# Decoder block on one core: the product of the triangular inverse with the scores, cut to the 64 rows that are used

## The reference, cut to what matters

```python
def step(S, inp):
    qt, kt, vt, gt, bt = inp
    S = S * jnp.exp(gt)[..., None, None]
    kv = jnp.einsum('bhk,bhkv->bhv', kt, S)
    delta = (vt - kv) * bt[..., None]
    S = S + jnp.einsum('bhk,bhv->bhkv', kt, delta)
    o = jnp.einsum('bhk,bhkv->bhv', qt, S)
    return (S, o)
```

## Time and profile before

| | before |
|---|---|
| time, median of 3 executions | 2269.97 us (2269.26 to 2271.44) |
| span of the profiled execution, first to last instruction | 2267.6 us |
| mean granted TensorE clock | 0.981 |
| PE busy | 2108.4 us (93%) |
| DVE busy | 1704.1 us (75%) |
| ACT busy | 1397.1 us (62%) |
| POOL busy | 833.0 us (37%) |

### The profile page before, as it was taken

How to read it: one execution, slowest core, us unless ns; L and a number is a source line. 1 busy time by engine, 2 the same in 40 slices (tenths; PEclk the granted TensorE clock), 3 DMA queues, 4 the chain that set the end, 5 groups by cost and what they waited for, 6 DMA issues and landing times.

```text
span 2267.6 us, 81281 instructions
## 1 busy us (share of the span) xinstructions
PE 2108.4 (93%) x33098; PEld 1786.0 (79%) x33130; DVE 1704.1 (75%) x5291; ACT 1397.1 (62%) x4262; POOL 833.0 (37%) x1845
## 2 busy tenths in 40 slices
PE   4899999999999999999999999999999999999976
PEld 3688888788888888888888788878888878887864
DVE  4577777777777777878777778777778777777743
ACT  3575556776556776555776555776555776555642
POOL 3333334433334433334433334433334433334421
PEclk8799999999999999999999999999999999999997
DMA  6000000000000000000000000000000000000000
GB/s 226 7 2 10 10 10 9 9 3 10 10 10 9 10 2 10 10 10 10 9 2 10 10 10 10 9 2 10 10 10 10 9 2 10 10 10 10 7 4 3
DMA packets 25795, 30.66 MB, mean 14 GB/s; under 512 B 9264, under 2 KB 22592, under 8 KB 24656
## 3 DMA queue, kind: packets, MB, share of 16 engines
q1 hardware_dynamic: 25424, 25.46, 3.5%
HBM read 21.25 MB, written 4.19 MB: 11 GB/s over the span
## 4 chain that ended last, share of the span: by engine, by line
PE 46%; DVE 25%; ACT 18%; POOL 6%; issue 5%; DVEq 0%; POOLq 0%
PE bank_b L644 10%; ACT prob L934 6%; PE bank_a L464 5%; PE bank_b L746 5%; PE bank_b L652 5%; DVE acc L1021 5%; PE bank_a L546 4%; DVE u L1097 3%; DVE y1p L1150 3%; PE bank_a L536 3%; DVE diag L1057 2%; POOL ostat L1387 2%; DVE bn L1109 2%; ACT L862 2%; DVE kkT L1038 2%
## 5 line engine op out<-in xcount | busy, mean ns | idle before, releaser
L1021 DVE SCALAR_TENSOR_TENSOR acc<-ypad,convw,acc 128x128 f32<-128x128 f32 x1536 | 469.5, 376 | 111.2 <-ACT acc L823 111.2
L464 PE MATMUL bank_a<-xnT,wqkvz 128*128 128x128 f32 x2048 | 250.9, 279 | 25.0 <-DVE u L1097 25.0
L464 PEld LDWEIGHTS bank_a<-xnT,wqkvz 128*128 128x128 f32 x2048 | 240.6, 195 | 37.5 <-issue 37.5
L1433 POOL TENSOR_SCALAR lnv<-mv 128x1 f32<-128x1 f32 x128 | 24.6, 193 | 603.3 <-DVE mv L1111 600.7
L1387 POOL TENSOR_TENSOR ostat<-ostat 128x4 f32<-128x4 f32 x64 | 52.6, 822 | 488.4 <-ACT gseg L888 488.4
L934 ACT ACTIVATE prob<-bank_b,nmax 128x128 f32<-128x128 f32 x512 | 182.4, 382 | 4.4 <-DVE nmax L1171 1.8
L815 ACT ACTIVATE xnT<-bank_a 128x256 f32<-128x256 f32 x32 | 12.3, 385 | 231.3 <-PE bank_a L451 231.3
L536 PE MATMUL bank_a<-zblk,kkT 32*32 32x32 f32 x8192 | 122.9, 195 | 31.8 <-DVE zblk L1081 19.3
L823 ACT ACTIVATE acc<-bank_a,convw 128x128 f32<-128x128 f32 x512 | 148.2, 398 | 0.0
L536 PEld LDWEIGHTS bank_a<-zblk,kkT 32*32 32x32 f32 x8192 | 98.9, 106 | 51.2 <-issue 50.1
L746 PE MATMUL bank_b<-y2T,wc 128*128 128x128 f32 x1024 | 133.1, 285 | 0.0
(11 more groups left out here) (253 smaller groups left out, 5626.9 us busy)
## 6 DMA issues: line engine op xcount, KB each, us to landing
xin<-in_x_dram SPq DMA_DIRECT2D x32, 128.0 KB, 2.2
cin<-in_ctx_dram SPq DMA_DIRECT2D x32, 128.0 KB, 2.0
out_dram<-yout SPq DMA_DIRECT2D x32, 128.0 KB, 2.9
wqkvz<-in_wqkvz_dram SPq DMA_DIRECT2D x6, 512.0 KB, 6.7
wout<-in_wout_dram SPq DMA_DIRECT2D x1, 1024.0 KB, 9.4
wg<-in_wg_dram SPq DMA_DIRECT2D x1, 1024.0 KB, 11.1
wu<-in_wu_dram SPq DMA_DIRECT2D x1, 1024.0 KB, 13.1
wd<-in_wd_dram SPq DMA_DIRECT2D x1, 1024.0 KB, 14.6
```

Of the source, the lines that this page charges most:

```text
L464: last = mm(A[bank][:, b * P:(b + 1) * P], wqkvz[:, c, o:o + P], xnT[:, c, :], start=(c == 0), stop=(c == KC - 1))
L1021: stt(acc[:, c, :], ypad[:, c, k:k + P], convw[:, c, k:k + 1], acc[:, c, :], ALU.mult, ALU.add).then_inc(conv.sem, 1)
```

## The change

The product is computed only for the columns of `zfull` that give rows 0 to 63 of the result, so the stationary operand has 64 columns in place of 128. The heads of a half are taken in pairs: the even head's result goes to partitions 0 to 63 of the bank, the odd head's to partitions 64 to 127 of the same 128 columns, so that the two use the two column halves of the array. Four heads fill 256 columns of the bank, not 512. ACT copies with two instructions of 64 partitions by 256 elements: one for the even heads, from partitions 0 to 63, and one for the odd heads, from partitions 64 to 127 of the bank to partitions 0 to 63 of `scoreT`. The semaphore is raised by the second. The number of matmuls and of their moving columns is the same.

```diff
                 pe.wait_ge(*u_ok(n, 1 + half)).then_inc(pe_passed.sem, 1)
-                for b in range(4):
-                    h = 4 * half + b
-                    last = mm(A[1 + half][:, b * P:(b + 1) * P], zfull[:, h, :], scoreT[:, h, :], start=True, stop=True)
+                for b in range(2):
+                    for odd, side in enumerate((TOP, BOT)):
+                        h = 4 * half + 2 * b + odd
+                        last = mm(A[1 + half][side, b * P:(b + 1) * P], zfull[:, h, TOP], scoreT[:, h, :], start=True, stop=True)
                 last.then_inc(sz_ps.sem, 1)
 
             def score_z(n, half):
                 act.wait_ge(*sz_ps(n, 1 + half))
-                fn(scoreT[TOP, 4 * half:4 * half + 4, :], quad(A[1 + half])[TOP, :, :], ACT.Copy).then_inc(sz_ok.sem, 1)
+                for odd, side in enumerate((TOP, BOT)):
+                    last = fn(scoreT[TOP, 4 * half + odd:4 * half + 4:2, :], quad(A[1 + half])[side, 0:2, :], ACT.Copy)
+                last.then_inc(sz_ok.sem, 1)
```

## The result

| | before | after |
|---|---|---|
| time, median of 4 executions each | 2269.64 us (2269.26 to 2271.44) | 2279.34 us (2273.80 to 2282.89) |
| ratio | | 1.0041 (1.0029 to 1.0053) |
| span of the profiled execution | 2267.6 us | 2272.0 us |
| mean granted TensorE clock | 0.981 | 0.983 |

The change makes the kernel 9.7 us slower, 0.41%, and the interval is clear of 1; 2280 was forecast against a median of 2269.97.

A forecast was written before the change was run, and what follows sets the result against it. The chain at the edited step was taken to be on ACT, not PE: PE's saving 0, first copy +9.9 us, second copy 0, on a span of 2267.6 plus 2.4, giving 2280 us; range 2271 to 2287.

The forecast's parts named there:

- The bound: Around the edited step the chain runs over ACT, POOL and DVE; PE's saved 0.46 us per trip only lengthens its waits.
- the rival's: PE's saving reaches the end: chain shorter by 0.46 x 31 = 14 us, 2258 even with ACT's +2.2; chance 0.06.
- ACT's queue: ACT takes up half 0's copy at its own list's pace, so the product's earlier result gains nothing.
- the earlier sz_ps: PE's semaphore for the product's result comes 0.35 us earlier; without ACT's queue worth up to 11 us.
- The product's price: New product on PE: 0.66 us per half against 0.89, saving 0.23 per half, 0.46 per trip.
- The copies' price: On ACT, 0.80 us from first copy to next exponential, against 0.48: +0.32 per half, held by the moved source.
- the bounds: ACT's two copies: +0.07 per half if the destination decides (rival, 2272, chance 0.15), +0.32 if the source is enough.
- The sum: PE 0, first copy 31 x 0.32 = +9.9 us, second copy 0: span 2277.5, time 2280.
- The second half: a_sz1's copy adds 0.32 to 0.4 to ACT at no cost; of 0.64 us before a_core1, 0.2 to 0.3 stay spare.
- PE's new wait: About 1.0 us of new PE idle time per trip in front of a_o1's L589.
- PE's idle time: Up to a_qkv2, 0.81 us before, to grow by 0.46 + 0.32 = 0.78 per trip.

The follow-up runs named there:

- run 1: The changed 64-column product with the single copy of the kernel before, against the kernel before: 2264.62 us against 2266.55, ratio 0.9992.
- run 8: The changed kernel with half 0's two copies moved from ACT to DVE, against the kernel before: 2260.75 us, ratio 0.9958.
- 3: The kernel before with its copy cut in two, both from partitions 0 to 63 to partitions 0 to 63: ratio 1.0013 to the kernel before.
- 5: The kernel before with two copies, both read from partitions 0 to 63, the second written to partitions 64 to 127: ratio 1.0043 to the kernel before.
- run 2: The product of the kernel before with the change's two copies, against the kernel before: 2278.84 us, ratio 1.0059.
- 4: The changed kernel measured again, against the kernel before: 2278.22 us, ratio 1.0051.
- 6: The changed kernel with its two copies in the other order, odd heads first, against the kernel before: ratio 1.0037.
- run 9: Product and copies changed in half 0 alone, half 1 as before, against the kernel before: ratio 1.0046.
- run 10: Product and copies changed in half 1 alone, half 0 as before, against the kernel before: ratio 1.0002.

## Why the prediction was right

- **The bound.** That PE's saving is worth nothing because the chain is on ACT there: run 1 measures it, 0.08% where 0.6% was the rival's. The cover named was ACT's queue; run 8 takes half 0's copies out of it and the first half's saving appears. It appears at L820, through the earlier end of a_qkv0, and not through the earlier sz_ps, which the prediction had priced at 0.35 us.
- **The product's price.** This term was too small. 0.66 us per half was worked out from L718 and L526; 0.78 is measured in the second half. The 0.13 taken from L718 ends at L708's first record, and the way out also makes the first record of the next line slow, 0.10 us at L464. The row of L708 had shown some of it: 0.44 us for two records, where 0.11 + 0.28 = 0.39 would do. So the second half saves 0.11 us and not 0.23. That the sum per trip, 0.39, comes near the 0.46 is luck: the product of before cost 0.97 in the first half, not 0.89. The total was put at nothing at the end, so the forecast doesn't hang on it.
- **The copies' price.** 0.80 us from the first copy to the next exponential was forecast and 0.80 measured (0.79 in the median of 31 trips). The choice between the bounds went by likeness, in agreement with the rule of the Trainium skill for VectorE named there; runs 3 and 5 now show that either side's move holds and that two instructions without a move cost 0.05, not 0.07.
- **The sum.** 31 x 0.32 = 9.9 us was forecast; 9.7 was measured in the medians (0.29% to 0.53%), 0.51% in the repeat. The trips carry it: 16.21 to 16.54 us up to a_qkv2, and 16.52 to 16.55 in all runs in which half 0's held copies are on ACT (2, 4, 5, 6, 9), for whatever else they change. That the medians agree with the sum to 0.2 us is luck, with intervals some 5 us wide.
- **The second half.** Costed at nothing, measured +0.02% (run 10). The cover named was 0.64 us in front of a_core1, of which 0.2 to 0.3 were to be left; 0.38 are. The place of PE's new wait was wrong: about 1.0 us was expected in front of a_o1, but most of it, 0.54 in the trip shown, stands one step ahead, in front of c_pT3. That step waits for the exponentials that the first copy had made late, which I had left out of the list of those who wait. It takes both parts of the change: with the product alone (run 1) or the copies alone (run 2) PE's wait there stays at 29.2 and 28.8 us, where it was 28.7, and with both it is 44.0. It costs nothing, because PE waited at a_qkv2 anyway. That wait fell from 25.0 to 16.8 us, as foreseen, and it is half 1's late copies that shorten it: it is 15.6 us with half 1 changed alone (run 10), 26.7 with half 0 alone (run 9). PE's idle time grew by 0.26 us per trip in the profile, not 0.78; the rest is counted as busy, as said above.
- **Not foreseen:** the scatter of the changed kernel's executions, 9 us where the one before had 2 in the first measurement. On other chips the kernel before scattered as much (2263.99 to 2272.51 in 21 executions), so it says nothing on the change.

## What to carry to other kernels

Find out which engine the chain is on where the edited step stands, before pricing what another engine saves there; here 12 us of PE's time were worth nothing, and the 0.32 us per trip on ACT everything. On ACT, a copy that starts at another partition than the instruction before it, on either side, is paid at its own start and at the start of the next instruction, so put it on an engine, and at a place, where that one has idle time: the same product with half 0's copies on DVE is 0.42% and 0.44% faster than the kernel before in two measurements. Price a change of the array's shape up to the second record of the next line, since a part of it lies in the first.

## What the runs showed of the hardware that I had not expected

POOL's first scale took 1.48 us in nearly all trips before, for 128x4 elements, and 0.26 us in one (start us, us):

```profile
1158.56 1.48 POOL L1387 TENSOR_TENSOR ostat<-ostat 128x4 f32<-128x4 f32 x1 [14.63 <-ACT gseg L888]
...
1225.88 0.26 POOL L1387 TENSOR_TENSOR ostat<-ostat 128x4 f32<-128x4 f32 x1 [14.63 <-ACT gseg L888]
```

DVE was in the middle of the convolution's twelve instructions both times. In the long cases POOL's instruction ended some 0.06 us after the last of them; it had started some 0.245 us after the start of a DVE instruction, in the short case 0.157. The start alone doesn't settle it: in the first trip it was 0.01 us, and that case is long too (1.45 us). The second half's scale starts among such instructions as well and takes 0.25 us. No experiment looked into it.
